# Latent attention: the exponentials multiplied by Pool instead of VectorE, the weight split between items

## The chip, the cores and the metric

One core of a Trainium2 chip runs the whole program. The time is the device time of one execution in microseconds (us), lower is better; the median of three executions stands for a kernel. The core has a matrix engine (TensorE, PE in the profile, its weight loads PEld), a vector engine (VectorE, DVE), a scalar engine (ScalarE, ACT), GpSimd (Pool, POOL) and SyncE (SP), which only issues DMAs here. Each takes its own instructions in program order and waits for the others at semaphores. SBUF is the memory on the chip; TensorE writes into the eight banks of PSUM, and Pool works on SBUF alone.

## What is computed

Two layers, each an attention and a feed-forward part, on x of 16 x 100 x 512. The change touches only the first attention, a latent one with 16 heads over a context of 16 x 361 x 128. Cut to it:

```python
def _L0_xattn_ref(hidden_q, kv_c, Wq, w_kc_q, w_kc_kv, W_qr, W_kr, Wo):
    q_hk = (hidden_q @ Wq.T).reshape(Bv, Sv, H, K)
    q_big = jnp.einsum('bshk,hkq->bshq', q_hk, w_kc_q)
    q_big = _apply_rope(q_big, sin_q[None, :, None, :], cos_q[None, :, None, :])
    kv_r = _apply_rope(kv_c, sin_k[None], cos_k[None])
    q_r = jnp.einsum('bshq,hqr->bhsr', q_big, W_qr)
    k_r = jnp.einsum('bld,hdr->bhlr', kv_r, W_kr)
    scores = jnp.einsum('bhsr,bhlr->bhsl', q_r, k_r)
    attn = jax.nn.softmax(scores, axis=-1)
    ctx_c = jnp.einsum('bhsl,bld->bhsd', attn, kv_r)
    ctx_lat = jnp.einsum('bhsd,hkd->bhsk', ctx_c, w_kc_kv)
    ctx = ctx_lat.transpose(0, 2, 1, 3).reshape(Bv, Sv, H * K)
    return ctx @ Wo.T
```

The rest (quantised feed-forward, a causal attention, a mixture of experts) follows in the same program and is the same in both kernels.

## The kernel before

**Tiling.** The batch is taken in two halves of 8, the heads in 8 pairs: 16 runs (n = 0 to 15) of one pair on one half. Runs 0 and 8 start a half. A run has four units u (two blocks of 400 query rows, two heads) and 16 items j (8 batch entries, two heads).

**A run on TensorE** (`pair(n)` of the tensor block): it widens the queries to 384 columns (`widen`, L371) and projects the last two units (`project`, L355), narrows block 0 (`narrow(n, 0, 0, 1)`, L386), widens on, absorbs the key weights (`absorb`, L399), and then goes through 23 slots s. Slot s computes the scores of item s (L414) and transposes the probabilities of item s - 2 (`turn_probs`, L423). In between lie the last two widenings (slots 0 and 1), `narrow` of block 1 in two parts (slots 3 and 4), `absorb` of block 1 (slot 5), the mix with the values (L434) in each second slot from 5 on, the output (L447) from 8 on, and in slots 17 and 21 the first projections of the next run, which need its split weights.

**Precision.** Large products are made from a high part in fp32r and the rest as a low part. The weights of a run, Wq (128 x 1024) and Wkc (128 x 768), are split on Pool by four instructions (`split(n)`, L288 to L298): high part, and low part from it, of each.

**Rope of the queries.** VectorE multiplies each widened block by cosine and sine (`rope`, L683). The rotation's partner is added on Pool (`partners(n, u)`, two instructions of L263). `narrow` of block 0 waits for the partners of units 0 and 1, `narrow` of block 1 for those of units 2 and 3.

**An item's softmax.** VectorE takes the row maximum (L736), ScalarE the exponential with the row sum (L588), VectorE the reciprocal of the sum (L741) and the multiplication of the 100 x 361 exponentials by it (L743), both one slot after the scores; TensorE transposes, ScalarE copies the transpose (L606). The exponentials have four buffers.

**Pool's order.** Run 0: the kv rotation of the first half (`rotate`, L273 to L282, four instructions for each of eight entries) with partners 0 to 3 of run 0 between. Then for each run n from 1 on: `split(n)`, at n = 8 also `rotate(1, ...)` for the second half, then the partners of its four units. As Pool gets to `split(n)` when the last partners of run n - 1 are added, it works on it in the first slots of run n - 1. The second half's context lands in the weight buffer that run 7 has used, and SP loads the weights of run 9 there once Pool has rotated all of it.

Of the kernel before, what the change touches and what calls it, by code (L numbers as in the profile page):

```python
# [14 lines left out]
F32 = mybir.dt.float32  # L15
# [7 lines left out]
L, DC = 361, 128  # L23
# [101 lines left out]
def latent_attention(core, x_in, ctx_in, g_x, g_f, w_pack, rope_q, rope_k):  # L125
# [4 lines left out]
    with ExitStack() as own:  # L130
# [71 lines left out]
        def starts_half(n):  # L202
            return n % PAIRS == 0
# [4 lines left out]
        def loads(n):  # L208

            return 16 * (n // 2 + 1)  # L210
# [16 lines left out]
        with nc.Block() as block:  # L227
# [18 lines left out]
            def _(pool):  # L246
# [37 lines left out]
                def split(n):  # L284
                    w = wview(n)
                    pool.wait_ge(w_in[n % 2], loads(n))
                    pool.wait_ge(a_psum, n * UNITS)
                    pool.tensor_tensor(wqh[:].rearrange("p k c -> p (k c)"), w["q"],  # L288
                                       core.zero[:, 0:1].to_broadcast([128, KC * 256]), ALU.add).then_inc(w_high, 1)
                    pool.wait_ge(w_high, n * 2 + 1)  # L290
                    pool.tensor_tensor(wql[:].rearrange("p k c -> p (k c)"), w["q"],
                                       wqh[:].rearrange("p k c -> p (k c)").bitcast(F32),
                                       ALU.subtract).then_inc(w_split, 1)
                    pool.wait_ge(b_psum, n * UNITS * CB)
                    pool.tensor_tensor(wch[:], w["kc"], core.zero[:, 0:1].to_broadcast([128, 2 * CQ]),
                                       ALU.add).then_inc(w_high, 1)
                    pool.wait_ge(w_high, n * 2 + 2)
                    pool.tensor_tensor(wcl[:], w["kc"], wch[:].bitcast(F32),  # L298
                                       ALU.subtract).then_inc(w_split, 1)
# [8 lines left out]
                partners(0, 3)  # L308
                for n in range(1, RUNS):
                    split(n)  # L310
                    if starts_half(n):
                        rotate(1, range(HB))
                    for u in range(UNITS):
                        partners(n, u)
# [331 lines left out]
            def _(dve):  # L646
# [58 lines left out]
                def pair(n):  # L705
# [27 lines left out]
                    for s in range(SLOTS):  # L733
# [4 lines left out]
                        if 1 <= s < ITEMS + 1:  # L738
# [3 lines left out]
                            dve.wait_ge(s_rec, n * ITEMS + j + 1)  # L742
                            dve.tensor_scalar(prob[:, j % 4, 0:L], prob[:, j % 4, 0:L],  # L743
                                              rsum[:, j % 4:j % 4 + 1], None, ALU.mult).then_inc(s_norm, 1)
# [1668 lines left out]
```

## Time and profile before

| what | value |
|---|---|
| median of 3 runs | 2117.43 us (2115.23 to 2124.33) |
| the profiled execution | 2123.64 us, its span 2121.9 us |
| busy over the span | PE 1877.3 us (88%), DVE 1428.5 (67%), ACT 944.4 (45%), POOL 669.6 (32%) |
| latent attention | the first 1030 us or so, 16 runs |
| mean granted TensorE clock | 0.954 of full speed |

The span is the time from the first to the last instruction on the core; the execution's own time is 1.7 us longer. All durations below are of that one execution. A line such as L743 is a line of the kernel before; the changed kernel has other line numbers below L283. A row of the timeline with x8 holds eight like instructions of one engine, and a bracket at its end says how long the engine stood idle before it and what ended that.

### The profile page before, as it was taken

What the parts mean: (1) busy time and instruction counts of PE and PEld (TensorE: products, weight loads), DVE (VectorE), ACT (ScalarE), POOL (GpSimd) and SP (SyncE); (2) the same over time, 40 slices, a digit from 0 to 9 for tenths busy, and PEclk for the clock granted to TensorE, in tenths of its full rate; (3) what the DMA queues carried; (4) which work ended last, traced back from release to release, by engine and by line L of the source; (5) the groups of instructions that cost most, each with busy time, mean ns of one, the idle gap of its engine ahead of it and who ended that gap; (6) DMA issues with size and microseconds to landing.
All of it is one profiled execution on the core that took longest, in us unless ns stands there. A gap on an engine that the chain in (4) does not pass through costs nothing. (4 is left out here: it accounts for less than half of the span.)

```text
span 2121.9 us, 31624 instructions
## 1 busy us (share of the span) xinstructions
PE 1877.3 (88%) x11466; PEld 1489.5 (70%) x11466; DVE 1428.5 (67%) x2714; ACT 944.4 (45%) x1971; POOL 669.6 (32%) x620
## 2 busy tenths in 40 slices
PE   4899999999999999999427998899868899999997
PEld 4677778877678877777314554666545789999996
DVE  5777776778776777776677777477645535666664
ACT  3433333444433344433483332555425236666663
POOL 4322222226421222221113000232222464555553
PEclk9999999999999999999758999899978999999999
DMA  4111001110101110100321000000022347777774
GB/s 194 37 37 37 7 31 37 37 37 31 67 6 37 37 37 37 37 1 1 159 90 59 0 0 0 1 1 2 1 76 100 103 87 209 238 237 234 235 234 87
DMA packets 31106, 153.59 MB, mean 72 GB/s; under 512 B 5468, under 2 KB 5468, under 8 KB 20084
## 3 DMA queue, kind: packets, MB, share of 16 engines
q1 hardware_dynamic: 19268, 128.33, 16.6%
q0 software_dynamic: 11408, 23.37, 6.0%
q8 instruction: 88, 1.44, 0.3%
q14 instruction: 54, 0.44, 0.1%
q10 hardware_dynamic: 288, 0.00, 0.0%
HBM read 131.17 MB, written 20.51 MB: 71 GB/s over the span
## 5 line engine op out<-in xcount | busy, mean ns | idle before, releaser
L263 POOL TENSOR_TENSOR la_q_roped<-la_q_roped 128x400 f32<-128x400 f32 x128 | 132.6, 1056 | 668.4 <-DVE la_q_roped L683 668.4
L588 ACT ACTIVATE la_probs<-banks,la_minus_max 100x361 f32<-100x361 f32 x256 | 144.5, 564 | 196.5 <-DVE la_minus_max L736 196.5
L683 DVE TENSOR_TENSOR la_q_roped<-banks,la_rope_q 128x400 f32<-128x400 f32 x384 | 196.8, 566 | 30.9 <-PE banks L386 15.1
L1877 DVE TENSOR_TENSOR ex_weights_low<-ex_raw_weights,ex_weights_high 128x2048 fp32r<-128x2048 f32 x60 | 137.6, 2294 | 51.4 <-ACT ex_weights_high L1772 48.8
L423 PEld LDWEIGHTS banks<-identity,la_probs 100*121 100x121 f32 x768 | 113.1, 184 | 70.8 <-DVE la_probs L743 44.7
L743 DVE TENSOR_SCALAR la_probs<-la_probs,la_rsum 100x361 f32<-100x361 f32 x256 | 154.1, 602 | 9.1
L1030 PE MATMUL banks<-qf_sign_weights,qf_x_quant_t 128*100 128x512 bf16 x512 | 122.2, 389 | 33.0 <-DVE qf_hidden L1111 18.6
L434 PE MATMUL banks<-la_probs_t,la_kv_rows 121*128 121x200 f32 x768 | 151.3, 332 | 0.0
L736 DVE TENSOR_REDUCE la_minus_max<-banks 100x1 f32<-100x361 f32 x256 | 135.0, 527 | 16.2 <-PE banks L414 9.6
L423 PE MATMUL banks<-identity,la_probs 100*121 100x100 f32 x768 | 126.0, 273 | 21.2 <-DVE la_probs L743 18.3
L2144 POOL TENSOR_TENSOR ex_g_low<-ex_g,ex_g_high 128x256 fp32r<-128x256 f32 (+1 forms) x104 | 86.5, 948 | 180.9 <-ACT ex_g_high L1816 180.5
L434 PEld LDWEIGHTS banks<-la_probs_t,la_kv_rows 121*128 121x128 f32 x768 | 131.5, 189 | 1.8
L1772 ACT CAST ex_weights_high<-ex_raw_weights 128x2048 fp32r<-128x2048 f32 x60 | 114.3, 1905 | 39.8 <-PE banks L2225 37.4
L606 ACT COPY la_probs_t<-banks 121x300 f32<-121x300 f32 x256 | 105.5, 412 | 53.4 <-PE banks L423 53.2
L543 ACT CAST la_q_high<-banks 128x400 fp32r<-128x400 f32 x64 | 31.6, 493 | 215.1 <-PE banks L355 215.1
L2188 PE MATMUL banks<-ex_block_t_high,ex_weights_high 128*128 128x256 f32 (+1 forms) x416 | 118.8, 286 | 4.0 <-DVE ex_block_t_low L1883 2.4
L1030 PEld LDWEIGHTS banks<-qf_sign_weights,qf_x_quant_t 128*100 (+1 forms) x512 | 63.1, 128 | 82.7 <-DVE qf_hidden L1111 25.1
L2209 PE MATMUL banks<-ex_u_high,ex_weights_high 128*128 128x256 f32 (+1 forms) x416 | 120.4, 289 | 0.7 <-ACT ex_silu_gate L1813 0.7
L762 DVE TENSOR_TENSOR residual<-residual,banks 100x512 f32<-100x512 f32 x128 | 88.0, 687 | 45.2 <-PE banks L447 43.5
L2209 PE MATMUL banks<-ex_u_low,ex_weights_high 128*128 128x256 f32 (+1 forms) x416 | 118.1, 284 | 0.0
L2188 PE MATMUL banks<-ex_block_t_high,ex_weights_low 128*128 128x256 f32 (+1 forms) x416 | 118.0, 284 | 0.0
L2188 PE MATMUL banks<-ex_block_t_low,ex_weights_high 128*128 128x256 f32 (+1 forms) x416 | 118.0, 284 | 0.0
(321 smaller groups left out, 5370.7 us busy)
## 6 DMA issues: line engine op xcount, KB each, us to landing
ex_raw_weights<-w_exp SPq DMA_DIRECT2D x60, 1024.0 KB, 4.9
la_weights<-w_pack SPq DMA_DIRECT2D x15, 1856.0 KB, 7.6
qf_raw_weights<-w_ffn SPq DMA_DIRECT2D x2, 4096.0 KB, 22.0
residual<-x SPq DMA_DIRECT2D x2, 2048.0 KB, 14.7
qf_raw_weights<-w_ffn SPq DMA_DIRECT2D x2, 2048.0 KB
out<-ex_block_out POOLq DMA_DIRECT2D x13, 256.0 KB, 4.0
normed_rows<-ex_xn SPq DMA_DIRECT2D x16, 200.0 KB
out<-residual SPq DMA_DIRECT2D x4, 800.0 KB
```

The lines of the kernel that those rows point to most:

```text
L263: pool.tensor_tensor(roped[:, h, 0, c, :], roped[:, h, 0, c, :], roped[:, h, 1, 1 - c, :], ALU.add).then_inc(b_add, 1)
L423: mm = pe.transpose(ps[0:LC, T_BANK, c * S:(c + 1) * S], prob[:, j % 4, c * LC:(c + 1) * LC], core.ident[0:S, 0:S])
L434: mm = pe.matmul(ps[:, V_BANK, 0:2 * S], kv[:, b, c, :], probt[:, b % 2, c, :, :].rearrange("p h s -> p (h s)"), start=(c == 0), stop=(c = ...
L588: act.activation(prob[:, s % 4, 0:L], ps[0:S, s % 2, 0:L], ACT.Exp, bias=nmax[:, s % 4:s % 4 + 1], accum_out=sums[:, s % 4:s % 4 + 1]).the ...
L683: dve.tensor_tensor(roped[:, h, v, c, :].rearrange("p (b s) -> p b s", b=GB), ps[:, B_BANKS[k % 2], 0:NT].rearrange("p (b s) -> p b s", b=GB),
L736: dve.tensor_reduce(nmax[:, s % 4:s % 4 + 1], ps[0:S, s % 2, 0:L], AX.X, ALU.max, negate=True).then_inc(s_max, 1)
L743: dve.tensor_scalar(prob[:, j % 4, 0:L], prob[:, j % 4, 0:L], rsum[:, j % 4:j % 4 + 1], None, ALU.mult).then_inc(s_norm, 1)
L1030: mm = pe.matmul(ps[0:S, bank + c % 2, :], xqt[:, k, bass.ds(t * S, S)], wq[:, m, k * DI + c * 512:k * DI + (c + 1) * 512], start=(k == 0) ...
L1772: act.copy(wh[:, m, :], raw[:, m, :]).then_inc(w_high[m], 1)
L1877: dve.tensor_tensor(wl[:, m, :], raw[:, m, :], wh[:, m, :].bitcast(F32), ALU.subtract).then_inc(w_low[m], 1)
L2188: mm = pe.matmul(upb(j, c, n), mat((wh, wl)[a], UP)[:, k, c * 128:(c + 1) * 128], (xbh, xbl)[x][:, j % 2, k, 0:n], start=(k == 0 and i == ...
L2209: mm = pe.matmul(gateb(c, n), mat((wh, wl)[a], GATE)[:, k, c * 128:(c + 1) * 128], (uh, ul)[x][:, k, 0:n], start=(k == 0 and i == 0), stop ...
```

## The change

VectorE keeps the reciprocal and leaves out the multiplication. Pool makes it, as a tensor_scalar on the same tile (`normalise(n, j)`), after waiting for the reciprocal of that item. So Pool goes along with the items: `pair(n)` on Pool first adds the partners of units 0 to 2 (in run 0 they stand ahead as before), then multiplies item 0, adds the partners of unit 3, and multiplies items 1 to 15. The split of the next run's weights is cut in its four instructions; they stand behind the multiplications of items 4, 6, 8 and 10. The rotation of the second half stands ahead of `pair(8)`.

```diff
+                def normalise(n, j):
+                    pool.wait_ge(s_rec, n * ITEMS + j + 1)
+                    pool.tensor_scalar(prob[:, j % 4, 0:L], prob[:, j % 4, 0:L],
+                                       rsum[:, j % 4:j % 4 + 1], None, ALU.mult).then_inc(s_norm, 1)
...
-                def split(n):
+                def split_q(n, low):
...
+                def split_c(n, low):
...
+                def pair(n):
+                    if n:
+                        for u in range(UNITS - 1):
+                            partners(n, u)
+                    for j in range(ITEMS):
+                        normalise(n, j)
+                        if j == 0:
+                            partners(n, UNITS - 1)
+                        if n + 1 < RUNS:
+                            if j in (4, 6):
+                                split_q(n + 1, j == 6)
+                            if j in (8, 10):
+                                split_c(n + 1, j == 10)
...
-                partners(0, 3)
-                for n in range(1, RUNS):
-                    split(n)
-                    if starts_half(n):
+                for n in range(RUNS):
+                    if n and starts_half(n):
                         rotate(1, range(HB))
-                    for u in range(UNITS):
-                        partners(n, u)
+                    pair(n)
...
                             dve.reciprocal(rsum[:, j % 4:j % 4 + 1], sums[:, j % 4:j % 4 + 1]).then_inc(s_rec, 1)
-                            dve.wait_ge(s_rec, n * ITEMS + j + 1)
-                            dve.tensor_scalar(prob[:, j % 4, 0:L], prob[:, j % 4, 0:L],
-                                              rsum[:, j % 4:j % 4 + 1], None, ALU.mult).then_inc(s_norm, 1)
```

`split_q(n, low)` and `split_c(n, low)` hold the same instructions and waits as `split(n)` did, `low` choosing the second of each couple.

Pool in an ordinary run, before, from the partners of a run (x8, four units) over the split of the next weights (la_wq, la_wkc) to the next partners:

```order
L263 TENSOR_TENSOR la_q_roped<-la_q_roped 128x400 x8
L288 TENSOR_TENSOR la_wq_high<-la_weights,zero 128x1024
L291 TENSOR_TENSOR la_wq_low<-la_weights,la_wq_high 128x1024
L295 TENSOR_TENSOR la_wkc_high<-la_weights,zero 128x768
L298 TENSOR_TENSOR la_wkc_low<-la_weights,la_wkc_high 128x768
```

Pool in the same place of the changed kernel, L286 being the multiplication:

```order
L263 TENSOR_TENSOR la_q_roped<-la_q_roped 128x400 x6
L286 TENSOR_SCALAR la_probs<-la_probs,la_rsum 100x361
L263 TENSOR_TENSOR la_q_roped<-la_q_roped 128x400 x2
L286 TENSOR_SCALAR la_probs<-la_probs,la_rsum 100x361 x4
L295 TENSOR_TENSOR la_wq_high<-la_weights,zero 128x1024
L286 TENSOR_SCALAR la_probs<-la_probs,la_rsum 100x361 x2
L299 TENSOR_TENSOR la_wq_low<-la_weights,la_wq_high 128x1024
L286 TENSOR_SCALAR la_probs<-la_probs,la_rsum 100x361 x2
L306 TENSOR_TENSOR la_wkc_high<-la_weights,zero 128x768
L286 TENSOR_SCALAR la_probs<-la_probs,la_rsum 100x361 x2
L310 TENSOR_TENSOR la_wkc_low<-la_weights,la_wkc_high 128x768
L286 TENSOR_SCALAR la_probs<-la_probs,la_rsum 100x361 x5
```

The last two partner adds have moved behind item 0, and each part of the split behind an item.

Pool between runs 7 and 8, before: the rotation of the second half (L273 to L282, the first entry of eight and the last row shown) stands behind the split that it makes early in run 7.

```order
L298 TENSOR_TENSOR la_wkc_low<-la_weights,la_wkc_high 128x768
L273 TENSOR_TENSOR la_kv_turned<-la_weights,la_rope_k 121x3x64
L275 TENSOR_TENSOR la_kv_turned<-la_weights,la_rope_k 121x3x64
L278 TENSOR_TENSOR la_weights<-la_weights,la_rope_k 121x384
L282 TENSOR_TENSOR la_kv_rows<-la_weights,la_kv_turned 121x384
...
L282 TENSOR_TENSOR la_kv_rows<-la_weights,la_kv_turned 121x384
L263 TENSOR_TENSOR la_q_roped<-la_q_roped 128x400 x8
```

And after:

```order
L310 TENSOR_TENSOR la_wkc_low<-la_weights,la_wkc_high 128x768
L286 TENSOR_SCALAR la_probs<-la_probs,la_rsum 100x361 x5
L273 TENSOR_TENSOR la_kv_turned<-la_weights,la_rope_k 121x3x64
L275 TENSOR_TENSOR la_kv_turned<-la_weights,la_rope_k 121x3x64
L278 TENSOR_TENSOR la_weights<-la_weights,la_rope_k 121x384
L282 TENSOR_TENSOR la_kv_rows<-la_weights,la_kv_turned 121x384
...
L282 TENSOR_TENSOR la_kv_rows<-la_weights,la_kv_turned 121x384
L263 TENSOR_TENSOR la_q_roped<-la_q_roped 128x400 x6
```

The five multiplications of items 11 to 15 of run 7 now stand ahead of the rotation; the first partners of run 8 stand behind it in both.

## Rows read from the trace of the kernel before

**Rows 1.** Windows: busy us (and instructions) by engine, granted clock, DMA share, GB/s.

```profile
241.00:298.00 57.00, 54.99 (x302) 43.58 (x302) 41.21 (x93) 23.06 (x67) 14.14 (x11) 1.00 0.10 34
```

**Rows 2.** Who waited for whom, TensorE, the first 1030 us: total, times, longest.

```profile
PE banks L423 <- DVE la_probs L743: 18.3, 30, 0.8
PE banks L399 <- ACT la_q_rank L547: 5.0, 14, 0.4
```

**Rows 3.** Timeline of TensorE in run 6: start, duration, engine, line, operation.

```profile
425.72 2.91 PE L386 MATMUL banks<-la_q_roped,la_weights 128*64 128x400 f32 x16 [0.18 <-POOL la_q_roped L263]
...
436.46 0.56 PE L423 MATMUL banks<-identity,la_probs 100*121 100x100 f32 x3 [0.80 <-DVE la_probs L743]
...
437.45 1.56 PE L386 MATMUL banks<-la_q_roped,la_weights 128*64 128x400 f32 x8
439.41 0.56 PE L423 MATMUL banks<-identity,la_probs 100*121 100x100 f32 x3 [0.39 <-DVE la_probs L743]
...
444.32 0.94 PE L399 MATMUL banks<-la_q_rank,la_weights 64*128 64x400 f32 x4 [0.36 <-ACT la_q_rank L547]
445.19 0.56 PE L423 MATMUL banks<-identity,la_probs 100*121 100x100 f32 x3
```

**Rows 4.** By tile, la_probs: durations in ns (minimum/median/maximum), first and last start.

```profile
L743 DVE TENSOR_SCALAR la_probs<-la_probs,la_rsum x256: 407/409/1900, 70.2 to 1022.8; 100x361 f32<-100x361 f32 x128
```

**Rows 5.** Timeline of TensorE in the last run.

```profile
994.76 0.56 PE L423 MATMUL banks<-identity,la_probs 100*121 100x100 f32 x3 [0.80 <-DVE la_probs L743]
...
1002.60 0.56 PE L423 MATMUL banks<-identity,la_probs 100*121 100x100 f32 x3
```

**Rows 6.** Timeline of Pool at the start of the next stage.

```profile
1045.75 6.01 POOL L862 TENSOR_SCALAR qf_hidden<-residual,rstd,minus_mean_rstd 100x512 f32<-100x512 f32 x8 [12.01 <-DVE minus_mean_rstd L111]
```

**Rows 7.** By tile, la_weights: durations in ns.

```profile
L288 POOL TENSOR_TENSOR la_wq_high<-la_weights,zero x15: 1882/1891/1893, 71.9 to 934.8; 128x1024 fp32r<-128x1024 f32 x15
L291 POOL TENSOR_TENSOR la_wq_low<-la_weights,la_wq_high x15: 2357/2361/2367, 73.8 to 936.8; 128x1024 fp32r<-128x1024 f32 x15
L295 POOL TENSOR_TENSOR la_wkc_high<-la_weights,zero x15: 1567/1570/1575, 76.1 to 939.1; 128x768 fp32r<-128x768 f32 x15
```

**Rows 8.** Timeline of Pool in run 6.

```profile
423.52 2.05 POOL L263 TENSOR_TENSOR la_q_roped<-la_q_roped 128x400 f32<-128x400 f32 x2 [2.15 <-DVE la_q_roped L683]
...
435.15 2.13 POOL L263 TENSOR_TENSOR la_q_roped<-la_q_roped 128x400 f32<-128x400 f32 x2 [4.38 <-DVE la_q_roped L683]
```

**Rows 9.** Timeline of VectorE in run 6.

```profile
435.43 0.15 DVE L741 RECIPROCAL la_rsum<-la_sums 100x1 f32<-100x1 f32 x1
...
439.27 0.52 DVE L736 TENSOR_REDUCE la_minus_max<-banks 100x1 f32<-100x361 f32 x1
```

**Rows 10.** Timeline of TensorE in run 0.

```profile
69.55 0.38 PE L414 MATMUL banks<-la_kv_t_high,la_qk_high 128*100 128x362 f32 x1 [1.41 <-ACT la_probs L588]
...
71.06 0.74 PE L423 MATMUL banks<-identity,la_probs 100*121 100x100 f32 x3 [0.80 <-DVE la_probs L743]
...
72.64 2.57 PE L386 MATMUL banks<-la_q_roped,la_weights 128*64 128x400 f32 x8
```

**Rows 11.** Windows, run 0, granted clock in the third column from the right.

```profile
72.00:74.00 2.00, 2.00 (x7) 0.72 (x7) 1.96 (x4) 0.95 (x3) 1.92 (x2) 0.50 0.00 0
```

**Rows 12.** Timeline of run 6: VectorE's reciprocal of item 6, TensorE's load of item 7.

```profile
448.17 0.15 DVE L741 RECIPROCAL la_rsum<-la_sums 100x1 f32<-100x1 f32 x1
...
452.07 0.46 PEld L423 LDWEIGHTS banks<-identity,la_probs 100*121 100x121 f32 x3
```

**Rows 13.** Timeline from run 7 to run 8: Pool, VectorE, Pool, TensorE.

```profile
512.54 0.59 POOL L273 TENSOR_TENSOR la_kv_turned<-la_weights,la_rope_k 121x192 f32<-121x192 f32 x1 [6.69 <-DMA la_weights<-ctx_rows]
...
530.43 0.15 DVE L741 RECIPROCAL la_rsum<-la_sums 100x1 f32<-100x1 f32 x1
...
538.27 1.01 POOL L282 TENSOR_TENSOR la_kv_rows<-la_weights,la_kv_turned 121x384 f32<-121x384 f32 x1
...
555.12 2.91 PE L386 MATMUL banks<-la_q_roped,la_weights 128*64 128x400 f32 x16
```

More of the change, by code:

```diff
@@ L282, in rotate @@
                         pool.tensor_tensor(kv[:, b], src[:, b], t, ALU.add).then_inc(kv_roped, 1)
-                def split(n):
-                    w = wview(n)
[L286 to L299, printed above, removed]
@@ new lines, in normalise @@
+                def normalise(n, j):
[3 more added lines that the diff above has]
+                def split_q(n, low):
+                    w = wview(n)
+                    high_q = wqh[:].rearrange("p k c -> p (k c)")
+                    if not low:
+                        pool.wait_ge(w_in[n % 2], loads(n))
+                        pool.wait_ge(a_psum, n * UNITS)
+                        pool.tensor_tensor(high_q, w["q"], core.zero[:, 0:1].to_broadcast([128, KC * 256]),
+                                           ALU.add).then_inc(w_high, 1)
+                    else:
+                        pool.wait_ge(w_high, n * 2 + 1)
+                        pool.tensor_tensor(wql[:].rearrange("p k c -> p (k c)"), w["q"], high_q.bitcast(F32),
+                                           ALU.subtract).then_inc(w_split, 1)
@@ new lines, in split_c @@
+                def split_c(n, low):
+                    w = wview(n)
+                    if not low:
+                        pool.wait_ge(b_psum, n * UNITS * CB)
+                        pool.tensor_tensor(wch[:], w["kc"], core.zero[:, 0:1].to_broadcast([128, 2 * CQ]),
+                                           ALU.add).then_inc(w_high, 1)
+                    else:
+                        pool.wait_ge(w_high, n * 2 + 2)
+                        pool.tensor_tensor(wcl[:], w["kc"], wch[:].bitcast(F32),
+                                           ALU.subtract).then_inc(w_split, 1)
```

## The prediction

> **What bounds the kernel now.** I read the stage by its windows first, then TensorE's waits, then the timeline around them. Latent attention makes 16 runs in the first 1030 us of the span. In a quiet stretch of 57 us TensorE is busy 54.99, VectorE 41.21, Pool 14.14 [rows 1]: TensorE's own work sets the pace, and nothing that relieves VectorE can give more than the 2.0 us that are left. The waits say whose these are: 18.3 us in 30 waits for the multiplication that the change moves (L743), 5.0 us in 14 waits for ScalarE's copy of the rank block [rows 2]. In one run [rows 3]: item 0's transpose (436.46) waited 0.80 for L743, item 1's (439.41) 0.39, and the absorb step (444.32) 0.36 for ScalarE, which was late because VectorE was. Then no wait worth naming until the next run. So 1.55 us a run can be won at most, and only if no new wait comes.
>
> Why those two later waits exist: while Pool splits the next weights, L743 takes up to 1.90 us against its median 0.41 [rows 4]. In the last run Pool has nothing to split: from item 0's transpose to item 3's takes 1002.60 - 994.76 = 7.84 us there [rows 5] and 445.19 - 436.46 = 8.73 in the ordinary one [rows 3]. The split costs 0.89 us a run; 14 runs have it (the 14 waits of ScalarE's copy in [rows 2]).
>
> **Price of the moved instruction.** VectorE loses 256 multiplications [rows 4]; it bounds nothing, so this is worth nothing by itself. Pool gains 256 of a form not in this stage. Nearest rows [rows 6, 7]: a tensor_scalar on 512 columns, eight back to back in 6.01 us, 0.75 each; and how the price falls with columns, from a one-input split at 1024 and 768 columns, (1.891 - 1.570)/256 = 1.25 ns a column. So 0.75 - 151 x 1.25 ns = 0.56; by the single durations of 0.77 it would be 0.58. I take 0.60, since Pool must also write it home before anyone hears of it. The lower end is 0.50 (0.75 scaled by 361/512 is 0.53), the upper the 1.03 of a two-input partner add on 400 columns [rows 8].
>
> The Trainium skill, page "GPSIMD Engine Reference", section 3.1, puts a tight one-input loop at 1.8 cycles of 1.2 GHz an element and 512 elements at 769 ns; for 361 that is an estimate of 0.54 us. The 0.75 us of [rows 6] agrees within 3%. By that figure the sum below would be about 1 us smaller.
>
> **Term 1: the start of every run.** Pool runs in order. Today it adds the last partners (unit 3) as soon as they are there, 435.15 to 437.28 [rows 8]; the change puts them behind item 0's multiplication. That needs the reciprocal of item 0, over at 435.43 + 0.15 = 435.58 [rows 9], and VectorE does nothing before it that the change removes. So, with 0.08 for the handover: multiplication 435.66 to 436.26; two partner adds, together 2.05 [rows 8], until 438.31; TensorE hears of Pool 0.15 later (423.52 + 2.05 = 425.57 to 425.72, [rows 3, 8]). The narrow step, which waits for these partners, starts at 438.46 instead of 437.45 [rows 3], 1.01 late. From there nothing else is late: Pool does item 1 by 438.9, and TensorE asks for it 1.5 us after the narrow step began. The last run shows narrow-to-item-3 without waits: 7.84 - (437.45 - 436.46) = 6.85. Item 3's transpose: 438.46 + 6.85 = 445.31 against 445.19. One wait has taken the place of three: **+0.12 x 14 = +1.7 us**. In the last run nothing is given back, for L743 was not held up there after item 0: **+1.0**. Run 0 [rows 10]: reciprocal over at 71.06 - (436.46 - 435.58) = 70.18, narrow at 70.18 + 0.08 + 0.60 + 2.05 + 0.15 = 73.06 against 72.64, nothing given back: **+0.4**. Each 0.1 on Pool's price is 1.6 us in this term.
>
> **Term 2: the parts of the split between items.** They now follow items 4, 6, 8 and 10. The tightest is the low part of Wq (2.36, [rows 7]) ahead of item 7. Reciprocal of item 6 over at 448.17 + 0.15; then 0.08 + 0.60 + 2.36 + 0.60 and some 0.1 for a wait on itself end at 452.06. TensorE loads item 7 at 452.07 [rows 12]. VectorE works off one L743 (0.41) ahead of this reciprocal today, so I let it come 0.3 earlier: hidden, with 0.3 to spare. The other three parts are at least 0.47 shorter. The users of the split (slot 17 of the same run) stand 18 us later. **Zero**; with Pool at 1.03 an item it would be 2 x 0.43 - 0.3 = 0.56 a run, 8 us.
>
> **Term 3: the middle.** Run 8 starts the second half of the batch, and Pool first turns eight kv tiles. Today they lie behind the split, in the middle of run 7, 512.54 to 538.27 + 1.01 = 539.28, 26.74 us, beside TensorE's items; TensorE needs the partners of run 8 for its narrow step at 555.12 [rows 13]. Now they lie behind the multiplication of item 15 of run 7, whose reciprocal is over at 530.43 + 0.15 [rows 13]: this ends at 530.58 + 0.68 = 531.26, the tiles at 558.00, and behind them stand partners of units 0 and 1: 4.10 more, 562.10, with 0.15 for the handover 562.25. TensorE stands still for 7.1 us, and all that follows hangs on that narrow step: **+7.1**. Half a run used to lie beside the tiles; now only the 24.5 us from the reciprocal to narrow do, and the tiles with the partner adds want 31.5. The load of run 9's weights on SP waits for the same tiles, comes some 19 us later, and is wanted only at item 4 of run 8: zero. Lower end 6.5, if Pool turns tiles faster with VectorE quiet.
>
> **Term 4: TensorE's clock.** In run 0 TensorE stood 1.41 and 0.80 us, and then the granted clock was 0.50 between 72 and 74, the lower of its two levels, 1.2 GHz [rows 10, 11]. Item 0's transpose to the end of narrow took 72.64 + 2.57 - 71.06 = 4.15 there, 437.45 + 1.56 - 436.46 = 2.55 at full clock: one fall costs 1.6 us. The 7.1 us of term 3 are a far longer pause than those: **+1.6**. Bounds 0.8 and 3.
>
> Sum: 1.7 + 1.0 + 0.4 + 7.1 + 1.6 = **11.8 us**. The profiled execution took 2123.64 (its span 2121.9) and would become 2135.4. It lies 6.2 above the median 2117.43, which is the yardstick: 2117.43 + 11.8 = **2129.2**, 0.56% slower. About 0.5% (10.6 us) is what a measurement of this kernel can tell from no change.
>
> **Does the pair of engines get in each other's way?** The removed L743 is the only VectorE instruction here that Pool held up; the reduction over the scores keeps its 0.52 us at 439.27, while Pool splits [rows 9]. The Trainium skill, "Perfetto Trace Analysis", section "Optimizing Scalar/DVE Operations", warns that the two share an SBUF port, so moving work between them might not help. L743's 1.90 against 0.41 [rows 4] agrees that they block each other; the multiplication itself leaves the conflict, so no loss is booked for it.
>
> **Rivals.**
> (a) As reckoned, the clock falling once in the middle: 2129.2, between 2125 and 2134. Chance 0.52.
> (b) Slower by more: the clock also falls in ordinary runs. Their new wait of about 1.0 at narrow comes 1 us behind the one for item 0, 0.7, close to run 0's 1.41 and 0.80 [rows 10]; against it, 0.80 and 0.39 did not do it [rows 1, 3]. At 1.6 each: four runs, +6.4, 2135.6; all fourteen, +22.4, 2151.6. It decides from the point where the two waits together count like run 0's. Chance 0.2.
> (c) Cheap hand-overs: Pool 0.50 an item, the middle 6.5, the clock 0.8: 0.3 + 0.9 + 0.3 + 6.5 + 0.8 = 8.8, 2126.2, within the bound. Chance 0.2.
> (d) Faster: TensorE's 1.55 a run and L743's 0.80 in the runs 0 and 15 fall away and the narrow wait does not come, -23.3, and with terms 3 and 4 -14.6: 2102.8. It needs the partner adds done by 437.45, so Pool's item below 0 us by term 1, or narrow not to depend on them; only something about Pool's overlap that no row shows could do it. Chance 0.06.
> (e) The move does not relieve VectorE, because Pool's multiplications hold up other VectorE work. Each item in reach of TensorE would be late by up to 0.6; against it stands the unchanged reduction. With 0.2 in half of the items +26 us, 2155. Chance 0.02.
>
> **How the numbers follow.** Range for 8 in 10: from below (c) with the spread of a median, 2121, to (b) with a few falls, 2140; this leaves out (d), (e) and the far part of (b). Of (a) some 0.3 lies beyond the bound, 0.22 within. Slower 0.3 + 0.2 + 0.02 = 0.52; same 0.22 + 0.2 = 0.42; faster 0.06.
>
> **What the profile after would show.** Pool's multiplication at 0.55 to 0.65 us. TensorE's longest wait in the stage in run 8, some 7 us, released by Pool's partner adds, with a granted clock below 1.00 beside it. In every run one wait of about 1 us at narrow, released by Pool; the 0.39 at item 1 and 0.36 at absorb gone. Wrong would be: no wait at narrow (then term 1 falls), a middle under 5 us, half clock in ordinary runs (then (b)), or waits of TensorE at items 5 to 11 for Pool (then term 2).

## The result: 2.6% slower

| | before | after |
|---|---|---|
| median | 2117.01 us (2115.23 to 2124.33, 4 runs) | 2176.1 us (2174.17 to 2177.42, 4 runs) |
| profiled execution | 2123.64 us, span 2121.9 | 2174.17 us, span 2172.4 |
| ratio after/before | | 1.0263, 95% interval 1.024 to 1.0285 |
| forecast | | 2129.2, range 2121 to 2140 |

The changed kernel takes 59 us more, not 12. The direction was right, the size outside the range. The two profiled executions differ by 50.5 us only, since the one before lies 6.6 above its median. And the rest of the program, whose instructions are the same in all kernels here, takes between 1092 and 1105 us from one profiled execution to the next, counted from the stage's last exponential (1100.5 before, 1097.8 changed). So what a change does is read below from the length of the stage and of its runs, and differences of a few us in the totals are left open.

Two groups of the page (part 5: line, engine, operation, forms, count, busy us, mean ns, idle before) show what Pool's multiplication costs, in the place of [rows 4]:

```profile
L286 POOL TENSOR_SCALAR la_probs<-la_probs,la_rsum 100x361 f32<-100x361 f32 x256 | 303.6, 1192 | 184.8 <-DVE la_rsum L764 183.1
L263 POOL TENSOR_TENSOR la_q_roped<-la_q_roped 128x400 f32<-128x400 f32 x128 | 130.5, 1042 | 278.1 <-DVE la_q_roped L706 278.1
```

The same by tile (minimum/median/maximum in ns, then from when to when in us):

```profile
L286 POOL TENSOR_SCALAR la_probs<-la_probs,la_rsum x256: 1180/1192/1211, 70.3 to 1076.1; 100x361 f32<-100x361 f32 x128
```

Each multiplication took 1.19 us where 0.60 was forecast and 0.50 to 1.03 allowed. The 256 durations lie between 1.18 and 1.21, whatever VectorE does beside them, so the price is the instruction's own. TensorE's waits in the stage, against [rows 2]:

```profile
PE banks L446 <- POOL la_probs L286: 27.9, 33, 1.3
PE banks L409 <- POOL la_q_roped L263: 24.8, 31, 7.0
```

The waits for the multiplication have grown from 18.3 to 27.9 us, and those for Pool's partner adds from 2.7 to 24.8. Where they lie, the timeline of the changed kernel shows; Pool first, then TensorE in the same run (against [rows 3, 8]), then TensorE's narrow step in run 8 (against [rows 13]):

```profile
452.74 1.19 POOL L286 TENSOR_SCALAR la_probs<-la_probs,la_rsum 100x361 f32<-100x361 f32 x1 [4.90 <-DVE la_rsum L764]
453.89 2.02 POOL L263 TENSOR_TENSOR la_q_roped<-la_q_roped 128x400 f32<-128x400 f32 x2
455.89 2.36 POOL L286 TENSOR_SCALAR la_probs<-la_probs,la_rsum 100x361 f32<-100x361 f32 x2
...
464.85 2.36 POOL L286 TENSOR_SCALAR la_probs<-la_probs,la_rsum 100x361 f32<-100x361 f32 x2
467.18 2.39 POOL L299 TENSOR_TENSOR la_wq_low<-la_weights,la_wq_high 128x1024 fp32r<-128x1024 f32 x1
469.54 2.36 POOL L286 TENSOR_SCALAR la_probs<-la_probs,la_rsum 100x361 f32<-100x361 f32 x2
...
453.98 0.56 PE L446 MATMUL banks<-identity,la_probs 100*121 100x100 f32 x3 [1.28 <-POOL la_probs L286]
...
456.06 1.56 PE L409 MATMUL banks<-la_q_roped,la_weights 128*64 128x400 f32 x8 [1.02 <-POOL la_q_roped L263]
...
470.78 0.56 PE L446 MATMUL banks<-identity,la_probs 100*121 100x100 f32 x3 [0.42 <-POOL la_probs L286]
...
583.81 4.26 PE L409 MATMUL banks<-la_q_roped,la_weights 128*64 128x400 f32 x16 [7.02 <-POOL la_q_roped L263]
```

Item 0's transpose waits 1.28 us (0.80 before), the narrow step 1.02, and item 7's transpose waits 0.42 (470.78): from 464.85 to 471.9 Pool never pauses between multiplications and the low part of Wq. In run 8 the narrow step waits 7.02 us and then runs at a lower clock, 4.26 us for what took 2.91.

The length of a run, from its first exponential to that of the next, is what the rest is told in. It was 60.8 us in each ordinary run before (434.15 to 494.92, for one). In the changed kernel it is 62.6 in five of the thirteen ordinary runs, some 64.2 in seven, and 63.5 in run 8:

```profile
196.01 0.56 ACT L611 ACTIVATE la_probs<-banks,la_minus_max 100x361 f32<-100x361 f32 x1 [1.54 <-DVE la_minus_max L759]
...
260.22 0.56 ACT L611 ACTIVATE la_probs<-banks,la_minus_max 100x361 f32<-100x361 f32 x1 [1.54 <-DVE la_minus_max L759]
...
451.20 0.56 ACT L611 ACTIVATE la_probs<-banks,la_minus_max 100x361 f32<-100x361 f32 x1 [1.54 <-DVE la_minus_max L759]
...
513.80 0.56 ACT L611 ACTIVATE la_probs<-banks,la_minus_max 100x361 f32<-100x361 f32 x1 [1.54 <-DVE la_minus_max L759]
```

260.22 - 196.01 = 64.2, 513.80 - 451.20 = 62.6. The windows view tells the two apart (us; busy time by engine; the third column from the right is TensorE's granted clock), the first row being the first 62.6 us of the longer run, the second a piece of it, the others pieces of run 7, of the middle (from run 7 to run 8) and of the last run:

```profile
196.00:258.60 62.60, 59.44 (x313) 46.01 (x311) 33.64 (x79) 24.00 (x68) 34.41 (x28) 0.97 0.09 31
...
200.90:204.30 3.40, 3.40 (x11) 1.37 (x12) 0.25 (x1) 0.22 (x2) 2.16 (x2) 0.50 0.00 0
...
518.40:521.70 3.30, 3.05 (x9) 1.04 (x10) 0.53 (x1) 0.50 (x2) 2.44 (x3) 0.50 0.00 0
579.80:586.50 6.70, 2.69 (x8) 1.11 (x10) 1.05 (x2) 0.00 (x0) 3.86 (x4) 0.50 0.79 284
1047.40:1050.70 3.30, 3.30 (x12) 1.33 (x11) 0.14 (x1) 0.11 (x2) 2.06 (x2) 0.50 0.00 0
```

Right behind the two waits the granted clock fell to 0.50, 1.2 GHz, from 200.9 to 204.3 us, and that run is 1.6 us longer. The same happened in eight of the thirteen ordinary runs (2, 3, 5, 8, 9, 10, 12 and 13), at the start of run 7 and in the last run. From the first exponential of the stage to its last the changed kernel needs 53.2 us more: 35.5 in the thirteen ordinary runs (13 x 1.8 for the waits, the other 12 for eight falls of the clock), 11.2 from run 7's first exponential to run 8's (83.2 against 72.0), of which 1.6 is run 7's own fall, 3.2 in run 0, 3.3 in the last.

### The profile page after: what moved, and what is told of

It reads as the page before. It is cut to its first block and busy times, and to the rows that moved or that the text cites. A ratio compares the mean times of both kernels' runs of the same rounds, so it can differ in the third digit from the quotient of the medians.

```text
span 2172.4 us, 31624 instructions
## 1 busy us (share of the span) xinstructions
PE 1904.0 (88%) x11466; PEld 1495.7 (69%) x11466; DVE 1282.2 (59%) x2458; ACT 952.1 (44%) x1971; POOL 968.4 (45%) x876
## 5 line engine op out<-in xcount | busy, mean ns | idle before, releaser
L286 POOL TENSOR_SCALAR la_probs<-la_probs,la_rsum 100x361 f32<-100x361 f32 x256 | 303.6, 1192 | 184.8 <-DVE la_rsum L764 183.1
L446 PE MATMUL banks<-identity,la_probs 100*121 100x100 f32 x768 | 133.8, 284 | 29.5 <-POOL la_probs L286 27.9
L409 PE MATMUL banks<-la_q_roped,la_weights 128*64 128x400 f32 x512 | 110.6, 567 | 24.8 <-POOL la_q_roped L263 24.8
L2229 PE MATMUL banks<-ex_u_high,ex_weights_low 128*128 128x256 f32 (+1 forms) x416 | 118.4, 285 | 0.0
```

The lines of the kernel that those rows point to most:

```text
L286: pool.tensor_scalar(prob[:, j % 4, 0:L], prob[:, j % 4, 0:L], rsum[:, j % 4:j % 4 + 1], None, ALU.mult).then_inc(s_norm, 1)
L446: mm = pe.transpose(ps[0:LC, T_BANK, c * S:(c + 1) * S], prob[:, j % 4, c * LC:(c + 1) * LC], core.ident[0:S, 0:S])
L2229: mm = pe.matmul(gateb(c, n), mat((wh, wl)[a], GATE)[:, k, c * 128:(c + 1) * 128], (uh, ul)[x][:, k, 0:n], start=(k == 0 and i == 0), stop ...
```

## The experiments

Theory: one wrong price. The sum of the prediction would hold, but a Pool multiplication of this form costs 1.19 us, which makes the start of a run 0.6 us later, makes the split's parts late, and lengthens the waits so that the clock falls. Rivals: the order of the change is what costs, whoever multiplies; or the price is set by shape (361 is odd), by writing over its input, or by contention.

### Eight forms of the multiplication

```diff
-                    pool.tensor_scalar(prob[:, j % 4, 0:L], prob[:, j % 4, 0:L],
-                                       rsum[:, j % 4:j % 4 + 1], None, ALU.mult).then_inc(s_norm, 1)
+                    if f == 0:
+                        pool.tensor_scalar(p[:, 0:361], p[:, 0:361], r, None, ALU.mult).then_inc(s_norm, 1)
...
+                    if f == 3:
+                        pool.tensor_scalar(p[:, 0:361], p[:, 0:361], r, 0.0, ALU.mult, ALU.add).then_inc(s_norm, 1)
...
```

> The changed kernel with Pool's multiplication written in eight forms, one for each item number modulo 8, each on its own line (0: 361 columns as in the changed kernel, 1: 362 columns, 2: 364, 3: 361 with mult and then add 0.0, 4: 361 into another tile, 5: a tensor_tensor with the reciprocal spread over the columns, 6: 360 columns and then 1, 7: 364 with mult and add 0.0). The rows of the tile are 364 apart instead of 363. In the changed kernel each took 1.19 us where 0.60 was predicted from a tensor_scalar of 0.75 us on 512 columns. Theory A, the column count decides (361 is odd): forms 1, 2 and 7 take 0.55 to 0.60, form 6 0.75, forms 0, 3, 4 and 5 stay at 1.19. Theory B, the second operation decides (the row of 0.75 us had two operations, this one has one): forms 3 and 7 take 0.55 to 0.60, all other tensor_scalars 1.19. Theory C, writing over its own input decides: form 4 alone is short. If all tensor_scalars stay at 1.19, something else than shape and form decides.

By tile, durations in ns (minimum/median/maximum); L292 is form 0, L294 form 1, and so on in steps of two to L304 and L305 (form 6) and L307 (form 7):

```profile
L292 POOL TENSOR_SCALAR la_probs<-la_probs,la_rsum x32: 1199/1202/1224, 69.9 to 1041.2; 100x361 f32<-100x361 f32 x32
L294 POOL TENSOR_SCALAR la_probs<-la_probs,la_rsum x32: 1196/1201/1207, 73.1 to 1043.0; 100x362 f32<-100x362 f32 x32
L296 POOL TENSOR_SCALAR la_probs<-la_probs,la_rsum x32: 1197/1198/1205, 74.3 to 1045.1; 100x364 f32<-100x364 f32 x32
L298 POOL TENSOR_SCALAR la_probs<-la_probs,la_rsum x32: 567/571/581, 78.6 to 1047.0; 100x361 f32<-100x361 f32 x32
L300 POOL TENSOR_SCALAR la_probs_b<-la_probs,la_rsum x32: 1192/1193/1199, 81.0 to 1049.1; 100x361 f32<-100x361 f32 x32
L302 POOL TENSOR_TENSOR la_probs<-la_probs,la_rsum x32: 782/786/791, 84.0 to 1050.9; 100x361 f32<-100x361 f32 x32
L304 POOL TENSOR_SCALAR la_probs<-la_probs,la_rsum x32: 1183/1190/1192, 85.0 to 1053.1; 100x360 f32<-100x360 f32 x32
...
L307 POOL TENSOR_SCALAR la_probs<-la_probs,la_rsum x32: 562/568/579, 88.8 to 1054.6; 100x364 f32<-100x364 f32 x32
```

Theory B, alone: the two forms with a second operation take 0.57 us, all with one take 1.19 to 1.20, whatever the column count (360 to 364) and the target. Even a tensor_tensor with the reciprocal spread is quicker, 0.79. The row that the forecast scaled [rows 6] has two operations, and two column scalars.

### More forms, on a tile of their own

One instruction more behind each of items 0 to 10 of the two-operation kernel below, each with a semaphore of its own, for instance

```diff
+                    if j == 1:
+                        pool.tensor_scalar(e[:, 0:361], d[:, 0:361], r, None, ALU.add).then_inc(dum, 1)
...
+                    if j == 4:
+                        pool.tensor_scalar(e[:, 0:361], d[:, 0:361], 1.0, 0.0, ALU.mult, ALU.add).then_inc(dum, 1)
...
```

> The two-operation kernel with one instruction more behind each of items 0 to 10, on a tile of its own, only to be timed: one operation with the constant 1.0, one add of a column scalar, mult and add of two column scalars, mult by a column scalar and mult by 1.0, mult by 1.0 and add 0.0, a copy, one mult on 120 and 240 columns, two operations on 120 and 240 columns, one max; 361 columns where no number is said. Theory, the missing second operation makes it slow: all one-operation forms 1.19 at 361 columns, all two-operation forms 0.57, and one operation costs about 3.3 ns a column against 1.3. Rivals: the operation itself (mult slow, add and max not), or the column scalar (the constant form is short).

Medians by tile, in the order of the text on record:

| form | us |
|---|---|
| mult by the constant 1.0 | 1.134 |
| add of a column scalar | 1.206 |
| mult and add of two column scalars | 0.642 |
| mult by a column scalar, mult by 1.0 | 0.572 |
| mult by 1.0, add 0.0 | 0.496 |
| copy | 0.486 |
| one mult, 120 and 240 columns | 0.594, 0.889 |
| two operations, 120 and 240 columns | 0.369, 0.470 |
| one max | 1.198 |

It is neither the kind of operation nor where the scalar comes from. The third line is the form of [rows 6] itself: 0.64 at 361 columns, where the forecast had scaled it to 0.56. The 0.56 came close to the 0.57 of another form, with one column scalar and a constant, by luck. One operation costs (1.206 - 0.594)/241 = 2.5 ns a column, two (0.572 - 0.369)/241 = 0.84. The 3.3 and 1.3 ns expected were too high: both forms have a fixed part of some 0.27 to 0.29 us. Why the instruction that does less is the slower one no run here shows. Both runs with extra forms were executed once, and only durations are read from them.

### The changed kernel with the quick form

```diff
-                                       rsum[:, j % 4:j % 4 + 1], None, ALU.mult).then_inc(s_norm, 1)
+                                       rsum[:, j % 4:j % 4 + 1], 0.0, ALU.mult, ALU.add).then_inc(s_norm, 1)
```

> The changed kernel with Pool's multiplication in the form that took 0.57 us in the eight-form run: mult and then add 0.0, same tile, same 361 columns, same order. It tests the rest of the prediction, whose price was 0.60. Theory: with that price the prediction's sum holds: ordinary runs 60.8 to 61.0 us (60.8 before, 62.6 or 64.2 in the changed kernel), the middle 80 to 81 us (72.0 before), 2126 to 2131 us in all. Rival 1, the split's parts are late for TensorE at this price too: ordinary runs 61.3 or more, 2136 or more. Rival 2, the clock falls in ordinary runs at this price too (waits of 0.7 and 1.0 us): some runs 1.6 us longer than the others, 2135 to 2150.

2134.16 us (2133.63 to 2148.57, 6 runs) against 2124.95 of the kernel before beside it; ratio 1.0072, interval 1.0046 to 1.0099; two of the six executions took 2148, 14 us more than the other four. The total expected was 2126 to 2131. This is the test of all that the prediction said apart from the price. Its forecast of 1.0056 lies in the interval, but the stage, from first exponential to last, is 18.0 us longer than before, not 11.8. Timelines of TensorE in an ordinary run and in the middle, Pool between:

```profile
438.08 0.56 PE L446 MATMUL banks<-identity,la_probs 100*121 100x100 f32 x3 [0.65 <-POOL la_probs L286]
440.15 1.56 PE L409 MATMUL banks<-la_q_roped,la_weights 128*64 128x400 f32 x8 [1.01 <-POOL la_q_roped L263]
...
450.44 2.39 POOL L299 TENSOR_TENSOR la_wq_low<-la_weights,la_wq_high 128x1024 fp32r<-128x1024 f32 x1
452.81 0.57 POOL L286 TENSOR_SCALAR la_probs<-la_probs,la_rsum 100x361 f32<-100x361 f32 x1
...
565.11 4.97 PE L409 MATMUL banks<-la_q_roped,la_weights 128*64 128x400 f32 x16 [6.47 <-POOL la_q_roped L263]
```

Ordinary runs last 60.85 us (60.8 + 0.12 forecast), item 0 waits 0.65 and narrow 1.01, no item behind a part of the split waits (TensorE's waits for the multiplication are 10.5 us in 16), and the middle is 82.2. Four of the thirteen ordinary runs (4, 8, 11 and 13) are 1.4 to 1.6 us longer by a fall of the clock, and run 7 has one too, one stretch for all:

```profile
316.80:320.10 3.30, 3.12 (x9) 1.11 (x10) 0.46 (x1) 0.43 (x2) 1.13 (x3) 0.50 0.00 0
```

So rival 2 holds in part: the waits of 0.65 and 1.01 can bring the clock down too. These five falls, some 7.5 us, are more than the 6.2 us that the stage has above the forecast.

### Back to VectorE, in the order of the change

```diff
-                    pool.wait_ge(s_rec, n * ITEMS + j + 1)
-                    pool.tensor_scalar(prob[:, j % 4, 0:L], prob[:, j % 4, 0:L],
-                                       rsum[:, j % 4:j % 4 + 1], None, ALU.mult).then_inc(s_norm, 1)
+                    if j in (4, 6, 8, 10, 15):
+                        pool.wait_ge(s_norm, n * ITEMS + j + 1)
...
                             dve.reciprocal(rsum[:, j % 4:j % 4 + 1], sums[:, j % 4:j % 4 + 1]).then_inc(s_rec, 1)
+                            dve.wait_ge(s_rec, n * ITEMS + j + 1)
+                            dve.tensor_scalar(prob[:, j % 4, 0:L], prob[:, j % 4, 0:L],
+                                              rsum[:, j % 4:j % 4 + 1], None, ALU.mult).then_inc(s_norm, 1)
```

> The changed kernel with the multiplication back on VectorE; Pool's order stays that of the change: the split's parts behind items 4, 6, 8 and 10 (it waits there for VectorE's multiplication of that item), the rotation of the second half behind item 15. Theory A, the price of Pool's multiplication made nearly all of the loss beyond the 11.8 us predicted: ordinary runs come back to 60 to 61 us from one run's first exponential to the next run's, the middle stays 9 us longer than in the kernel before, and the total is 2117 + 5 to 15 us. Rival, the order of the split's parts makes the loss whoever multiplies: ordinary runs stay at 62.6 us or more and the total at 2145 or more.

2119.96 us against 2116.64, ratio 1.0002 (0.9985 to 1.0019). Ordinary runs are 59.9 us, a little below what I expected and 0.9 below the kernel before; the middle is 79.5 (72.0 before). The clock falls in no ordinary run. So the order of the change has two parts of opposite sign: the spread split gives 0.9 us a run, the 0.89 that the prediction read as the cost of the split [rows 3, 5], and the middle, with the late rotation, takes 7.5 us back. The stage is 4.4 us shorter than before; the totals do not show it.

### The split cut to 8 columns

The four parts of the split in the changed kernel work on 8 columns each, in this manner:

```diff
-                        pool.tensor_tensor(wch[:], w["kc"], core.zero[:, 0:1].to_broadcast([128, 2 * CQ]),
+                        pool.tensor_tensor(wch[:, 0:8], w["kc"][:, 0:8], core.zero[:, 0:1].to_broadcast([128, 8]),
```

> The changed kernel with the four parts of the split cut to 8 columns each, so that the weights of runs 1 to 15 are mostly stale and the result is not the reference's; Pool's multiplications of 1.19 us stay. It measures what the parts cost between the items. Theory A, Pool's items and parts together are late for TensorE (two multiplications and the low part of Wq are 4.8 us against the 4.1 us of two slots): ordinary runs shorten from 62.6 to 61.5 or 61.6 us, the total falls by 15 to 18 us. Rival, the parts are hidden and the loss sits in the start of the run alone: no change beyond 3 us. The clock's falls stay in both, since their waits lie at the start of the run.

2150.33 us, ratio 1.0146 (1.0112 to 1.018) against 1.0263 of the changed kernel: 25 us less, where 15 to 18 were expected. Ordinary runs are 61.5 to 61.6, as expected: 0.75 us above 60.8 is the start of the run with 1.19 us an item, 1.05 were the late parts. The transposes of run 6 in the two kernels tell where these 1.05 lie: 0.15 at item 5, 0.6 at item 7 behind the low part of Wq, the rest at items 8, 11 and 12. The expectation on the clock was wrong, and that is the other 10 us: TensorE's two waits at the start of a run are the same (1.3 and 1.0), yet the clock fell in run 0, in the middle and in the two runs behind it, and in no other. The waits make a fall possible; what decides in which run it comes was not settled.

### Run 8 in the order of run 0

```diff
+                    if n and starts_half(n):
+                        rotate(1, range(GB))
+                        partners(n, 0)
+                        rotate(1, range(GB, GB + 1))
+                        partners(n, 1)
+                        rotate(1, range(GB + 1, HB))
+                        partners(n, 2)
+                    elif n:
```

in place of the rotation ahead of `pair(8)`.

> The changed kernel with run 8 ordered on Pool as run 0 is: four of the eight kv entries rotated, partners of unit 0, one entry, partners of unit 1, three entries, partners of unit 2. TensorE's narrow step then waits for 17 us of rotation instead of 31. As predicted for the middle, its wait of 7.0 us for Pool's partner adds and the fall of the clock beside it disappear (7.0 + 1.6), and a wait of 2 to 4 us for the last kv entries comes: the total falls by 4 to 7 us. Rival, the wait only moves to the kv entries: 0 to 2 us.

In all the rival's case: 2175.4 us, ratio 1.0267 (1.0234 to 1.0301), no gain. The wait for the partners is gone, and in its place stand two for the last kv entries, 2.01 and 2.70 us:

```profile
582.84 0.53 PE L368 MATMUL banks<-identity,la_kv_rows 121*128 121x121 f32 x3 [2.01 <-POOL la_kv_rows L282]
586.08 0.86 PE L368 MATMUL banks<-identity,la_kv_rows 121*128 121x121 f32 x3 [2.70 <-POOL la_kv_rows L282]
```

The middle shortened from 83.2 to 79.7 us, but 1.6 of that is the fall of the clock in run 7, which did not come here; another ordinary run had one instead, nine of thirteen. The profiled stage is 3.4 us shorter than the changed kernel's, the executions are not. With the quick form the same order gave a middle of 80.9 against 82.2:

> The same, and run 8 ordered on Pool as run 0. In the changed kernel this order cut the middle from 83.2 to 79.8 us. Expected here: middle 3 to 4 us shorter than with the two-operation form alone, 2123 to 2128 us in all. If the middle's 7 us wait were no cost of its own (rival), no change.

2134.39 us, ratio 1.0048 (1.0033 to 1.0063); next to 1.0072 (1.0046 to 1.0099) no difference is proven. The middle is 1.4 us shorter where 3 to 4 were expected, and the total lies above the 2123 to 2128 expected.

### Only item 0 back on VectorE

In the two-operation kernel:

```diff
                     for j in range(ITEMS):
-                        normalise(n, j)
+                        if j:
+                            normalise(n, j)
                         if j == 0:
                             partners(n, UNITS - 1)
...
+                            if j == 0:
+                                dve.wait_ge(s_rec, n * ITEMS + 1)
+                                dve.tensor_scalar(prob[:, 0, 0:L], prob[:, 0, 0:L], rsum[:, 0:1], None,
+                                                  ALU.mult).then_inc(s_norm_first, 1)
```

TensorE waits on that semaphore for item 0.

> The two-operation kernel with item 0 of each run multiplied by VectorE (its one-operation form there), so that Pool adds the last partners at once; items 1 to 15 stay on Pool in the order of the change. Theory: the wait at narrow and the falls of the clock in ordinary runs hang on that one item: ordinary runs 59.9 us as in d1_dve (60.9 and sometimes 62.3 with item 0 on Pool), middle 79 to 81, the total equal to the kernel before within 3 us. Then Pool's other 240 multiplications cost and bring nothing. Rival: Pool's 15 items and the split's parts still delay TensorE somewhere: ordinary runs 60.3 or more.

2120.79 us against 2124.03, ratio 0.999 (0.9978 to 1.0003). Ordinary runs are 59.9 us, every one, with no fall of the clock. The middle is 79.7. TensorE's waits in the first 1090 us:

```profile
PE banks L451 <- DVE la_probs L772: 12.7, 16, 0.8
PE banks L411 <- POOL la_q_roped L264: 9.2, 15, 6.4
```

With the quick form, the one item ahead of the partner adds was the whole cost of the move in ordinary runs (60.85 against 59.9). And the other 240 multiplications on Pool bring nothing over d1_dve's order, which has the same 59.9 with all of them on VectorE: VectorE was not the bound.

### The partners ahead of item 0

```diff
+                    partners(n, UNITS - 1)
                     for j in range(ITEMS):
                         normalise(n, j)
-                        if j == 0:
-                            partners(n, UNITS - 1)
```

> The two-operation kernel with the partners of unit 3 ahead of item 0 on Pool instead of behind it. Theory: one of the two must wait for the other. The partners are then added some 0.5 us earlier than behind item 0, but item 0 is ready 1.5 us later, and TensorE takes item 0 first: ordinary runs 61.2 to 61.6 us where the two-operation kernel has 60.9, total 5 to 10 us above it. Rival: the wait at narrow was the dearer one: 60.6 or less.

2154.78 us, ratio 1.0147 (1.0125 to 1.0169). Where the clock stays, ordinary runs are 61.2 us, as reckoned; but item 0 now waits 2.13 us in one piece, the clock falls in six ordinary runs and in run 7, three of them 3.0 us longer instead of 1.6, and the total is 20 us above the two-operation kernel by the medians, 16 by the ratios, not 5 to 10.

### The best of both

VectorE multiplies, the split's parts stand behind items 4, 6, 8 and 10, and the rotation stands in run 7, behind the last part. Against d1_dve:

```diff
-                    if j in (4, 6, 8, 10, 15):
+                    if j in (4, 6, 8, 10):
                         pool.wait_ge(s_norm, n * ITEMS + j + 1)
...
+                        if n == PAIRS - 1 and j == 10:
+                            rotate(1, range(HB))
...
-                    if n and starts_half(n):
-                        rotate(1, range(HB))
```

> VectorE multiplies again, the split's parts stay behind items 4, 6, 8 and 10 as in d1_dve, and the rotation of the second half goes back into run 7, behind the last part of the split (item 10). d1_dve had ordinary runs of 59.9 us against 60.8 before, and lost the gain in the middle (79.5 against 72.0). Theory: only the spreading of the split is worth something, 0.9 us a run, and the late rotation is what ate it: here 59.9 us a run and a middle of 71 to 73, 2102 to 2107 us in all, faster than both kernels. Rival: the rotation beside VectorE's multiplications now costs what it saved, middle 76 or more, 2110 or more.

2113.84 us (2102.81 to 2114.48, 6 runs) against 2124.95 beside it (11 runs); ratio 0.9941, interval 0.9923 to 0.996: faster than both kernels. The expectation had named totals, 2102 to 2107 or 2110 and more, when the kernel before had run at 2117; beside this one it ran at 2125, so the runs inside decide. The profiled execution, one of two near 2104 while the other four took 2114, had ordinary runs of 59.9 and a middle of 71.2, as the theory said, the first exponentials of runs 7 and 8 in the timeline of ScalarE:

```profile
488.83 0.56 ACT L610 ACTIVATE la_probs<-banks,la_minus_max 100x361 f32<-100x361 f32 x1 [1.54 <-DVE la_minus_max L758]
...
560.02 0.56 ACT L610 ACTIVATE la_probs<-banks,la_minus_max 100x361 f32<-100x361 f32 x1 [1.54 <-DVE la_minus_max L758]
```

560.02 - 488.83 = 71.2. VectorE's multiplication in the same kernel, by tile:

```profile
L765 DVE TENSOR_SCALAR la_probs<-la_probs,la_rsum x256: 406/409/1359, 71.0 to 1009.7; 100x361 f32<-100x361 f32 x128
```

VectorE's multiplication is still held up beside the split, at items 7 and 11 (1.35 and 0.74 us in an ordinary run, 1.90 at most in [rows 4]), but there no wait of TensorE comes of it: its only one above 0.25 us in an ordinary run is that for item 0. The same 7.7 us of splitting cost 0.89 us at the start of a run and nothing in its middle. The stage is 13.9 us shorter than before: 11.5 in the thirteen ordinary runs, 0.8 in the middle, and 1.6 in run 0, where the clock did not fall this time.

## Why the prediction was wrong, step by step

**What bounds the kernel**: right. TensorE's waits at the start of a run were all there was to win; h1_first_on_vector and d1_dve win the same 0.9 us a run, and relieving VectorE of 240 multiplications adds nothing.

**Price of the moved instruction**: this is the step that failed. It took a row of the same operation name, a tensor_scalar of 0.75 us on 512 columns, and scaled it by columns, without asking whether the form was the same. That row has two operations, the new instruction one: it took 1.19 us, not 0.60. The slope of 1.25 ns a column came from yet another form, the split's tensor_tensor with zero spread; with two operations a tensor_scalar has 0.84, and the form of the row would take 0.64 at 361 columns, not 0.56. The upper end was wrong as well: 1.03, from a two-input add of 400 columns, looked like the dearer kind, and a one-operation tensor_scalar on 361 is dearer. The Trainium skill, page "GPSIMD Engine Reference", section 3.1, puts its tight loop at 1.8 cycles an element, an estimate of 0.54 us here; the total of the two-operation form is near it (0.57), its slope is not (0.84 ns a column against 1.5), and the one-operation form is far from it (1.19).

**Term 1, the start of a run**: the mechanism was right, and its formula too. The prediction gave 0.12 a run at 0.60 us and 1 us more for each us of price; at 1.19 that is 0.12 + 0.59 = 0.71, and s1_tiny shows 0.75. At 0.57 it is 0.09, and p1_twoop shows 0.05. The narrow step was forecast 1.01 late; counted from the run's first exponential it is 0.93 late in p1_twoop and 1.56 in the changed kernel, where the formula gives 1.60. For the last run 1.0 was forecast and for run 0 0.4; p1_twoop shows 0.96 and 0.1. In the changed kernel they grew by 3.3 and 3.2, with the wrong price and falls of the clock.

**Term 2, the split between items**: zero was right at the forecast price, as p1_twoop shows. At the true one it is 1.05 us a run. The prediction's own bound for 1.03 us an item was 0.56, and by the same formula 1.19 gives 2 x 0.59 - 0.3 = 0.88: the mis-sized term is again the price.

**Term 3, the middle**: 7.1 us of waiting forecast, 7.02 seen. That it fits so well is partly luck: with 1.19 for item 15 the same steps give 7.7, and in p1_twoop, near the forecast price, the wait was 6.47. The chain was right and some 0.6 too long.

**Term 4, the clock**: a fall in the middle forecast at 1.6 us, with bounds 0.8 and 3. Narrow there took 4.26 us instead of 2.91 in the changed kernel and 4.97 in p1_twoop. Terms 3 and 4 together were 8.7. Measured they are 11.2 less what run 7 lost by itself, 1.8 for the waits and 1.6 for its own fall: 7.8. In p1_twoop they are 10.2 - 0.1 - 1.5 = 8.6. What the term left out are the falls in other runs, at nothing in the sum and under rival (b).

**The two engines in each other's way**: right. VectorE's remaining instructions keep their durations (the row maximum has a median of 0.53 us, 0.52 before), and Pool's 1.19 is its own.

**Rival (b)**, 0.2, came true beside the wrong price: the clock fell in eight of the thirteen ordinary runs, 1.5 us each on average, where I had put the weight on none. It came true at the forecast price as well, in four ordinary runs of p1_twoop and in run 7. So the price was the main failure, but not the only one: with the right price the sum of 11.8 is still short of the stage's 18.0, by these falls.

In sum, with the right price the same steps give 0.71 x 14 + 0.88 x 14 = 22 for terms 1 and 2 in ordinary runs, 1.0 + 0.6 and 0.4 + 0.6 for the last and the first, 7.1 + 1.6 for the middle, and some 8 x 1.6 = 13 for the falls in ordinary runs: 46. Run 7, the last run and run 0 have one more stretch of low clock each, 4.8, and run 0 has the parts of a split too, 0.9: 52. The stage measured 53.

## What to carry to other kernels

Before scaling a duration, compare the whole form of the instruction (number of operations, kind of scalar, number of inputs), not its name and size; where the trace has no row of the very form, the upper end of its price must be wide, or the form must be written as the one that has a row. Work for an in-order engine that sits between others can be worth moving without moving it to another engine: putting the four parts of a split where the matrix engine has slack gave 0.6%, the move to Pool nothing. And a wait that merely replaces another can still cost the matrix engine's clock.

## What the runs showed of the hardware

- On Pool a tensor_scalar with one operation is slower than with two: 1.19 to 1.21 us against 0.57 on 100 x 361 f32 (0.64 with two column scalars), 2.5 against 0.84 ns a column; with the constant 1.0 as scalar 1.13 against 0.50. Mult, add and max do not differ. An idle second operation (add 0.0, mult by 1.0) halves the time.
- TensorE's granted clock went down to 0.50 behind two waits of 1.28 and 1.02 us in eight of the changed kernel's thirteen ordinary runs (from 200.9 to 204.3 us, for one), and behind 0.65 and 1.01 us in four of p1_twoop's, and cost about 1.6 us of the run each time; behind the same waits in s1_tiny it mostly stayed. In the ordinary runs of the kernel before, 0.80 and 0.39 us never brought it down.
